# The first four tiles routed by rank alone, and all sixteen low halves of the context subtracted by VectorE

## The chip, the cores and the metric

The kernel runs on one core of one Trainium2 chip. The metric is the time of one execution on the device in microseconds (us), as the median of three runs. The engines are named as the profile names them: PE is TensorE (PEld its weight loads), DVE is VectorE, ACT is ScalarE, POOL is GpSimd, SP is SyncE, whose queue issues most DMAs.

## What is computed

A gated cross-attention block whose attention is a mixture of four experts chosen by token id, followed by a second mixture of experts. `x` is 4 x 512 x 512 in fp32, so there are 2048 tokens; the context `ctx` is one 512 x 512 matrix for each of the four experts and serves as all three of its weights.

```python
def _L0_xattn_ref(hidden_states, token_ids, Wg, Wu, Wd):      # Wg = Wu = Wd = ctx_2048
    tid = jnp.clip(token_ids, 0, VOCAB - 1)
    expert_ids = jnp.minimum(tid // tokens_per_expert, E - 1)
    for e in range(E):
        g = jax.nn.silu(jnp.einsum('bsd,fd->bsf', hidden_states, Wg[e]))
        u = jnp.einsum('bsd,fd->bsf', hidden_states, Wu[e])
        y = jnp.einsum('bsf,df->bsd', g * u, Wd[e])
        out = jnp.where((expert_ids == e)[..., None], y, out)
...
x = x + jnp.tanh(g_xattn[0]) * _L0_xattn_ref(_layernorm(x, axis=-1), itok_BxS_13_99985, ctx_2048, ctx_2048, ctx_2048)
x = x + jnp.tanh(g_ffn[0]) * _L0_ffn_ref(_layernorm(x, axis=-1), L0_ffn_gate_W, L0_ffn_W1, L0_ffn_b1, L0_ffn_W2, L0_ffn_b2)
```

`_L0_ffn_ref` picks two of six small experts for each batch entry and adds their weighted outputs. The change does not touch it.

## The kernel before

**Routing.** The 2048 tokens are sorted by expert into 19 tiles of 128 rows. A chain of small DVE instructions computes for every token its rank within its expert (L498 to L511), from the rank its place in the tile (`pslot`) and its tile (`ptile`, L535 to L551), and two tables of ones and zeros: `slot_hot` (L530 on DVE, L404 on POOL: one compare of 128 columns for each of 16 groups of tokens) and `tile_hot` (L555, L559). PE multiplies the two (`invert`, L917); from the product DVE reads which row of `x` each place of each tile takes (L570 to L573), and a further three instructions (L564 to L567) give `te_i`, the expert of each tile. The semaphore `routed` says that this is done; POOL then gathers the tiles' rows from DRAM with indirect DMAs (L407) into a ring of six buffers, and SP passes on each landing as `x_ready`.

**The context.** Four DMAs of 1 MB bring it. PE transposes it in 16 parts of four transposes each (L988) into four banks in turn. ACT copies each part to the rounded high half `ctx_hi` (L800), and DVE subtracts it from the bank for the low half `ctx_lo` (L622), after which the bank is free for the fourth next part. For parts 0 and 1 PE transposes again and adds the negative of the high half with a matmul by `neg_ident` (L995, L997), and ACT copies the remainder as the low half (L796).

**A tile.** For tile j: `rows_statistics(j)` on DVE (L580 to L582), an inverse root on POOL (L412), `normalise(j)` on DVE, which writes the one buffer `h` (L597), `transpose_h(j)` on PE (L933), high half on ACT (`h_high`, L775), low half on DVE (`h_low`, L602), `first_product(j)` of 12 matmuls (L949), `silu_of(j)` on ACT (L785), `up(j)` on DVE (L614), `transpose_a(j)` (L940), `a_high` (L780) and `a_low` (L608), `second_product(j)` of 12 matmuls (L949), `residual(j)` on DVE (L588 to L592), and a scatter to DRAM by POOL (L418, L419). Each product reads high by high, high by low and low by high halves of the tile and the context.

**Order.** Each engine runs its own list, written out by hand. From tile 2 on PE repeats `tile_step(j)`: `transpose_a(j-1)`, `first_product(j)`, `transpose_h(j+1)`, `second_product(j-1)`; DVE repeats `a_low(j-1)`, `normalise(j+1)`, `residual(j-2)`, `h_low(j+1)`, `up(j)`, `rows_statistics(j+2)`. So `transpose_h(3)` stands in `tile_step(2)` and waits for `normalise(3)`. Ahead of that stands a prologue, with the routing, the context and tiles 0 and 1; it is what the change rewrites. The second mixture of experts follows the 19 tiles.

## Time and profile before

| what | value |
|---|---|
| median of three runs | 296.31 us (296.15 to 296.44) |
| the profiled execution | 296.44 us, of which 294.9 us are its span |
| granted clock of PE, mean | 0.998 |
| PE busy | 279.1 us, 95% of the span |
| DVE busy | 206.6 us, 70% |
| ACT busy | 108.2 us, 37% |
| POOL busy | 65.6 us, 22% |

Times inside the profile count from the start of its span. Busy time overlaps between neighbouring instructions of one engine; where a cost is needed, the distance from one instruction's start to the next one's is the better measure. The time of the execution is 1.5 us more than its span, which lies outside of the profile's instructions.

### The profile page before, as it was taken

How to read it: one execution, taken by the hardware profiler on the slowest of the kernel's cores; microseconds unless marked ns; L12 is line 12 of the kernel's file. 1: busy time of each engine (PE TensorE's matmuls, PEld its weight loads, DVE VectorE, ACT ScalarE, POOL GpSimd, SP SyncE). 2: the span in 40 equal slices, each digit the busy share in tenths (PEclk: the TensorE clock that was granted, in tenths of full speed). 3: DMA queues.
4: the chain of work that ended last, by engine and by line, in shares of the span. 5: the costliest groups of instructions: out<-in, count | busy, mean ns of one | idle time of the engine just before them, and what ended most of it. 6: DMA issues, size and time to landing. Idle time of an engine off the chain costs nothing.

```text
span 294.9 us, 4422 instructions
## 1 busy us (share of the span) xinstructions
PE 279.1 (95%) x1390; PEld 224.6 (76%) x1390; DVE 206.6 (70%) x457; ACT 108.2 (37%) x187; POOL 65.6 (22%) x93
## 2 busy tenths in 40 slices
PE   1977999999999999999999999999999999999995
PEld 0765888888888888877776878877788777878874
DVE  7897687887887899597769555686465854846133
ACT  1682223223223225353254272445442372442010
POOL 3541144545544555333240000000000000000000
PEclk9999999999999999999999999999999999999999
DMA  6941012223245322129515009650486205730003
GB/s 219 369 131 36 0 61 84 74 71 108 76 103 188 104 71 84 61 71 284 191 62 177 4 1 278 234 169 0 122 272 211 75 0 176 218 145 0 1 0 142
DMA packets 21489, 34.44 MB, mean 117 GB/s; under 512 B 1864, under 2 KB 10062, under 8 KB 21468
## 3 DMA queue, kind: packets, MB, share of 16 engines
q1 hardware_dynamic: 18400, 24.16, 25.2%
q0 software_dynamic: 3040, 9.98, 10.4%
q8 instruction: 12, 0.20, 0.3%
q14 instruction: 9, 0.07, 0.1%
q10 hardware_dynamic: 28, 0.02, 0.0%
HBM read 24.97 MB, written 9.19 MB: 116 GB/s over the span
## 4 chain that ended last, share of the span: by engine, by line
PE 84%; DVE 12%; DMA 1%; issue 1%; ACT 1%; POOL 0%; DVEq 0%; ACTq 0%; POOLq 0%; SPq 0%
PE bank L949 33%; PE bank L925 15%; PE bank L926 14%; PE bank L927 14%; PE bank L940 3%; PE bank L933 2%; PE bank L1031 2%; DVE ctx_lo L622 2%; DMA x_ring<-in_x,get_rows 1%; DVE x_odd L706 1%; DVE stats L580 1%; DVE w_lo L686 1%; DVE w_raw L530 1%; DVE a L614 1%; PE bank L1040 1%
## 5 line engine op out<-in xcount | busy, mean ns | idle before, releaser
L925 PE MATMUL bank<-w_lo,ctx_hi 128*128 128x512 f32 (+1 forms) x96 | 38.0, 395 | 0.4 <-DVE ctx_lo L699 0.4
L926 PE MATMUL bank<-w_hi,ctx_hi 128*128 128x512 f32 (+1 forms) x96 | 37.5, 390 | 0.0
L927 PE MATMUL bank<-w_hi,ctx_lo 128*128 128x512 f32 (+1 forms) x96 | 37.4, 390 | 0.0
L686 DVE TENSOR_TENSOR w_lo<-w_raw,w_hi 128x512 fp32r<-128x512 f32 (+2 forms) x24 | 27.7, 1173 | 3.9 <-ACT w_hi L836 3.9
L925 PE MATMUL bank<-ctx_lo,w_hi 128*128 128x512 f32 (+1 forms) x72 | 28.6, 397 | 0.0
L926 PE MATMUL bank<-ctx_hi,w_hi 128*128 128x512 f32 (+1 forms) x72 | 28.2, 392 | 0.0
L927 PE MATMUL bank<-ctx_hi,w_lo 128*128 128x512 f32 (+1 forms) x72 | 28.1, 391 | 0.0
L698 DVE TENSOR_SCALAR ctx_hi<-act,mix 128x512 fp32r<-128x512 f32 x16 | 7.8, 486 | 27.4 <-ACT act L844 27.4
L785 ACT ACTIVATE a<-bank 128x512 f32<-128x512 f32 x19 | 11.4, 598 | 42.6 <-PE bank L949 42.6
L844 ACT ACTIVATE act<-bank,b1T 128x512 f32<-128x512 f32 x16 | 10.9, 688 | 42.3 <-PE bank L927 41.0
L780 ACT ACTIVATE aT_hi<-bank 128x512 fp32r<-128x512 f32 x18 | 10.8, 598 | 41.7 <-PE bank L940 41.6
L836 ACT ACTIVATE w_hi<-w_raw 128x512 fp32r<-128x512 f32 (+2 forms) x24 | 23.6, 1016 | 4.1 <-DMA w_raw<-in_L_ffn_b 3.6
L949 PE MATMUL bank<-ctx_hi,hT_hi 128*128 x80 | 23.5, 416 | 1.4 <-ACT hT_hi L775 1.0
L949 PE MATMUL bank<-ctx_lo,hT_hi 128*128 x80 | 21.7, 392 | 0.3 <-DVE ctx_lo L622 0.3
L925 PEld LDWEIGHTS bank<-w_lo,ctx_hi 128*128 128x128 f32 (+1 forms) x96 | 18.0, 188 | 4.7 <-issue 0.9
L949 PE MATMUL bank<-ctx_hi,hT_lo 128*128 x80 | 21.5, 390 | 0.0
L418 POOL TENSOR_TENSOR x_ring<-x_ring,half 128x1 f32<-128x1 f32 x19 | 10.6, 556 | 48.2 <-DVE x_ring L592 48.2
L949 PE MATMUL bank<-ctx_hi,aT_hi 128*128 x72 | 21.1, 415 | 0.1
L608 DVE TENSOR_TENSOR aT_lo<-bank,aT_hi 128x512 fp32r<-128x512 f32 x18 | 12.3, 685 | 12.5 <-ACT aT_hi L780 12.5
L419 POOL DMA_INDIRECT x_scratch<-x_ring,put_rows x19 | 19.8, 1042 | 5.4 <-POOL x_ring L418 5.4
L927 PEld LDWEIGHTS bank<-w_hi,ctx_lo 128*128 128x128 f32 (+1 forms) x96 | 18.0, 188 | 3.8
L926 PEld LDWEIGHTS bank<-w_hi,ctx_hi 128*128 128x128 f32 (+1 forms) x96 | 18.1, 188 | 3.6
(167 smaller groups left out, 556.8 us busy)
## 6 DMA issues: line engine op xcount, KB each, us to landing
raw_ctx<-in_ctx SPq DMA_DIRECT2D x4, 1024.0 KB, 9.4
w_raw<-in_L_ffn_W SPq DMA_DIRECT2D x8, 512.0 KB
w_raw<-in_L_ffn_W SPq DMA_DIRECT2D x8, 448.0 KB, 4.7
x_even<-x_scratch SPq DMA_DIRECT2D x8, 257.0 KB, 3.5
x_odd<-x_scratch SPq DMA_DIRECT2D x8, 257.0 KB, 3.3
w_raw<-in_L_ffn_W SPq DMA_DIRECT2D x8, 256.0 KB, 3.7
out<-x_even SPq DMA_DIRECT2D x8, 256.0 KB, 2.3
out<-x_odd SPq DMA_DIRECT2D x8, 256.0 KB, 2.1
```

Of the source, the lines that this page charges most:

```text
L418: chain.run(pool.tensor_tensor(deviation, deviation, half[:, 0:1], ALU.pow), apart=True)
L419: pool.indirect_dma_start(x1_rows, bass.IndirectOffsetOnAxis(put_rows[:, j:j + 1], 0), x_ring[:, r * DS:(r + 1) * DS], None).then_inc(scat ...
L608: dve.tensor_tensor(lo[:, :, :].rearrange("p k t -> p (k t)"), bank[:, :], hi[:, :, :].rearrange("p k t -> p (k t)").bitcast(FP32), ALU.su ...
L686: dve.tensor_tensor(part_of(w_lo[s], piece), part_of(w_raw[s], piece), part_of(w_hi[s], piece).bitcast(FP32), ALU.subtract).then_inc(lo_do ...
L780: sc.activation(aT_hi[:, :, :].rearrange("p k t -> p (k t)"), aT_ps[:, :], ACT.Copy).then_inc(aT_hi_done, 1)
L785: sc.activation(a[:, :], z_ps[:, :], ACT.Silu).then_inc(silu_done, 1)
L836: sc.activation(part_of(w_hi[s], piece), part_of(w_raw[s], piece), ACT.Copy).then_inc(hi_done[s], 1)
L844: sc.activation(dst, hid_ps[k % 2][0:rows, :], ACT.Gelu, bias=b1T[0:rows, c, bass.ds(e, 1)]).then_inc(gelu_done, 1)
L925: pe.matmul(dst, s_hi, m_lo, start=first, stop=False)
L926: pe.matmul(dst, s_hi, m_hi, start=False, stop=False)
L927: return pe.matmul(dst, s_lo, m_hi, start=False, stop=last)
L949: return pe.matmul(dst[:, :], src[:, k, :], weights[:, bass.ds(e * (KD * F1) + k * F1, F1)], start=first, stop=last)
```

## The change

The first tile of each expert becomes tile 0 to 3, in the order of the experts, so that tile and expert follow from the rank alone. For it there are tables of their own: `first_slot` (13 compares on DVE, 3 on POOL) and `first_hot` (two DVE instructions), a first `invert`, and the semaphore `first_routed`, after which POOL gathers four tiles. The other 15 tiles are routed later, with `slot_hot` (12 compares on POOL, 4 on DVE), `tile_hot`, `te_i` and a second `invert` spread over the work on tiles 0 to 2. The products of tiles 0 and 1 begin before the context is complete: its transposes 10 to 15 now stand between PE's work on tiles 0 and 1. DVE makes all 16 low halves; the matmuls by `neg_ident` and ACT's two copies are gone. The small tables `gwT` and `b1T` are transposed ahead of the context and copied by ACT, no longer by DVE. Tile 1 gets buffers for its two halves and a bank of its own.

```diff
@@ PE: ahead of the loop
-            for n in range(E * KD):
-                if n == 2:
-                    invert()
-                if n == 8:
-                    turn_small_tables()
...
-            transpose_h(0)
-            pe.wait_ge(routed, 2)
-            e = expert_of(0)
-            pe.wait_ge(ctx_hi_done, E * KD)
...
-            first_product(0, e, low_context)
-            transpose_h(1)
+            spread_gates()
+            turn_small_tables()
+            transpose_ctx(0)
+            transpose_ctx(1)
+            transpose_ctx(2)
+            pe.wait_ge(first_slot_done, IDC)
+            pe.wait_ge(first_hot_done, 2)
+            invert(aT_ps, first_slot, first_hot, E).then_inc(first_rows_done, 1)
+            for n in range(3, 8):
+                transpose_ctx(n)
+            transpose_ctx(8)
+            transpose_ctx(9)
             transpose_h(0)
+            transpose_ctx(10)
+            first_product(0, 0, lambda: transpose_h(1))
+            transpose_ctx(11)
+            transpose_ctx(12)
+            first_product(1, 1)
+            transpose_a(0)
+            transpose_h(2)
+            transpose_ctx(13)
+            transpose_ctx(14)
+            second_product(0, 0)
+            transpose_ctx(15)
+            pe.wait_ge(slot_hot_done, IDC)
+            pe.wait_ge(tile_hot_done, 1)
+            pe.wait_ge(ctx_lo_done, 13)
+            invert(o_ps[0], slot_hot, tile_hot, LATER).then_inc(rows_done, 1)
...
-            tile_step(1)
@@ ACT
-            for n in range(E * KD):
-                sc.wait_ge(ctxT_done, n + 1)
...
-                if 1 <= n <= BY_ACT:
-                    split_low_alone(n - 1)
...
+            for n in range(0, 10):
+                ctx_high(n)
             h_high(0)
+            ctx_high(10)
+            h_high(1)
             silu_of(0)
-            h_high(1)
+            ctx_high(11)
+            ctx_high(12)
             a_high(0)
+            h_high(2)
             silu_of(1)
-            h_high(2)
+            ctx_high(13)
+            ctx_high(14)
+            ctx_high(15)
@@ DVE, after the rank
+            dve.wait_ge(rank_made, 1)
+            for c in range(FIRST_BY_POOL, IDC):
+                dve.tensor_scalar(first_slot[:, c, :], col_h[:, :], rank[:, c:c + 1], None, ALU.is_equal).then_inc(first_slot_done, 1)
...
+            dve.wait_ge(first_rows_done, 1)
+            rows_of(slice(0, E), aT_ps, E, first_routed)
...
+            ctx_low(0)
...
+            ctx_low(4)
...
+            rows_statistics(0)
+            ctx_low(5)
+            normalise(0)
+            rows_statistics(1)
+            ctx_low(6)
             dve.wait_ge(tg_done, 1)
             h_low(0)
             normalise(1)
...
+            h_low(1)
             up(0)
-            h_low(1)
             rows_statistics(2)
...
+            a_low(0)
+            h_low(2)
...
+            up(1)
+            for c in range(LATER_BY_POOL, IDC):
+                dve.tensor_scalar(slot_hot[:, c, :], col_h[:, :], pslot[:, c:c + 1], None, ALU.is_equal).then_inc(slot_hot_done, 1)
...
+            dve.wait_ge(rows_done, 1)
+            rows_of(slice(E, TILES), o_ps[0], LATER, routed)
+            ctx_low(15)
             dve.memset(act_last[:, :], 1.0).then_inc(pads_made, 1)
@@ POOL
+            pool.wait_ge(first_routed, 2)
+            for j in range(E):
+                gather(j, j)
+            inverse_root(0)
+            inverse_root(1)
+            pool.wait_ge(pslot_done, 1)
+            for c in range(LATER_BY_POOL):
+                if c == LATER_BY_POOL // 2:
+                    inverse_root(2)
+                pool.tensor_scalar(slot_hot[:, c, :], col_h[:, :], pslot[:, c:c + 1], None, ALU.is_equal).then_inc(slot_hot_done, 1)
+            inverse_root(E - 1)
             pool.wait_ge(routed, 2)
```

The order of DVE's list where the first tile comes in, before (from the end of the routing on):

```order
L573 CAST put_rows<-rows_f 128x19
L622 TENSOR_TENSOR ctx_lo<-bank,ctx_hi 128x512 [waits ctx_hi_done] x6
L580 BN_STATS stats<-x_ring 128x6 [waits x_ready]
L581 BN_AGGR mv<-stats 128x2 [waits dve_step]
L582 TENSOR_SCALAR ve<-mv 128x1 [waits dve_step]
L622 TENSOR_TENSOR ctx_lo<-bank,ctx_hi 128x512 [waits ctx_hi_done] x2
L597 TENSOR_SCALAR h<-x_ring,mv,rstd 128x512 [waits rstd_ready]
```

Ahead of the first statistics stand six low halves (parts 2 to 7), and eight follow. The same place of DVE's list after the change (`starts` belongs to the routing of the later tiles):

```order
L604 TENSOR_TENSOR ctx_lo<-bank,ctx_hi 128x512 [waits ctx_hi_done] x3
L620 TENSOR_TENSOR starts<-ends,ntile 128x8 [waits dve_step]
L564 BN_STATS stats<-x_ring 128x6 [waits x_ready]
L565 BN_AGGR mv<-stats 128x2 [waits dve_step]
L566 TENSOR_SCALAR ve<-mv 128x1 [waits dve_step]
L604 TENSOR_TENSOR ctx_lo<-bank,ctx_hi 128x512 [waits ctx_hi_done]
L581 TENSOR_SCALAR h<-x_ring,mv,rstd 128x512 [waits rstd_ready]
```

Five low halves (0 to 4) stand ahead of the first statistics now, and eleven follow. DVE's list between `up(1)` and `normalise(3)`, before (L608 is `a_low(1)`, the second L597 row is `normalise(3)`):

```order
L614 TENSOR_TENSOR a<-bank,a 128x512 [waits silu_done]
L580 BN_STATS stats<-x_ring 128x6 [waits x_ready]
L581 BN_AGGR mv<-stats 128x2 [waits dve_step]
L582 TENSOR_SCALAR ve<-mv 128x1 [waits dve_step]
L608 TENSOR_TENSOR aT_lo<-bank,aT_hi 128x512 [waits aT_hi_done]
L597 TENSOR_SCALAR h<-x_ring,mv,rstd 128x512 [waits hT_done,rstd_ready]
```

Twelve rows of the same stretch of DVE's list after the change; ahead of them stand four compares, behind them the rest of L550 to L553, one more low half, a memset, and only then `a_low(1)` and `normalise(3)`:

```order
L658 TENSOR_TENSOR w_raw<-col_h,ptile 128x16x15 [waits dve_step]
L660 TENSOR_TENSOR w_raw<-w_raw,token_h 128x16x15 [waits dve_step]
L604 TENSOR_TENSOR ctx_lo<-bank,ctx_hi 128x512 [waits ctx_hi_done]
L564 BN_STATS stats<-x_ring 128x6 [waits x_ready]
L565 BN_AGGR mv<-stats 128x2 [waits dve_step]
L566 TENSOR_SCALAR ve<-mv 128x1 [waits dve_step]
L664 TENSOR_TENSOR w_raw<-col,ends 128x120
L604 TENSOR_TENSOR ctx_lo<-bank,ctx_hi 128x512 [waits ctx_hi_done]
L668 TENSOR_REDUCE te<-w_raw 128x15 [waits dve_step]
L604 TENSOR_TENSOR ctx_lo<-bank,ctx_hi 128x512 [waits ctx_hi_done]
L671 SCALAR_TENSOR_TENSOR te_i<-w_raw,te 128x15 [waits dve_step]
L550 SCALAR_TENSOR_TENSOR unused<-bank,slot 128x15 [waits rows_done,dve_step]
```

Between `up(1)` and `normalise(3)` there were two steps (statistics and `a_low(1)`); now the whole second half of the routing and the last four low halves lie between them as well. PE's list around the first product, before (L988 are the last two context parts, L933 is `transpose_h(0)`):

```order
L988 MATMUL bank<-ident,raw_ctx 128x128 [waits ctx_lo_done]
L988 MATMUL bank<-ident,raw_ctx 128x128 x3
L933 MATMUL bank<-ident,h 128x128 [waits h_ready]
L933 MATMUL bank<-ident,h 128x128 x3
L944 TENSOR_LOAD te_i [waits routed]
L944 ISA x2
L949 ISA [waits hT_hi_done,ctx_hi_done]
L949 MATMUL bank<-ctx_hi,hT_hi 128x512
```

The same place of PE's list after the change (L1033 is a context part, L972 a `transpose_h`, L990 a product; the first row is context part 9):

```order
L1033 MATMUL bank<-ident,raw_ctx 128x128 [waits ctx_lo_done]
L1033 MATMUL bank<-ident,raw_ctx 128x128 x3
L972 MATMUL bank<-ident,h 128x128 [waits h_ready]
L972 MATMUL bank<-ident,h 128x128 x3
L1033 MATMUL bank<-ident,raw_ctx 128x128 [waits ctx_lo_done]
L1033 MATMUL bank<-ident,raw_ctx 128x128 x3
L990 MATMUL bank<-ctx_hi,hT_hi 128x512 [waits ctx_hi_done,hT_hi_done]
L990 MATMUL bank<-ctx_hi,hT_hi 128x512 x3
L990 MATMUL bank<-ctx_lo,hT_hi 128x512 [waits ctx_lo_done]
L990 MATMUL bank<-ctx_lo,hT_hi 128x512 x3
```

`transpose_h(0)` stands behind ten context parts where it stood behind sixteen, and the first product behind eleven.

## Rows read from the trace of the kernel before

**Rows 1.** Page, part 4: the chain that ended last, shares by engine

```profile
PE 84%; DVE 12%; DMA 1%; issue 1%; ACT 1%; POOL 0%; DVEq 0%; ACTq 0%; POOLq 0%; SPq 0%
```

**Rows 2.** Chain of waits, 11 to 40 us: start us, us, what

```profile
12.12 4.32 DMA x_ring<-in_x,get_rows
...
27.58 0.66 PE bank L940 x4
28.24 2.75 PE bank L949 x12
...
34.62 2.76 PE bank L949 x12
37.38 0.44 PE bank L933 x4
```

**Rows 3.** Busy time of each engine by stretches, us (x instructions), granted clock

```profile
20.90:27.60 6.70, 4.43 (x24) 3.08 (x22) 4.98 (x15) 2.49 (x5) 1.56 (x2) 1.00 0.16 58
...
34.00:40.40 6.40, 6.40 (x33) 5.29 (x32) 5.07 (x12) 1.68 (x3) 2.14 (x3) 1.00 0.00 0
```

**Rows 4.** Timeline of DVE, 12 to 37 us: start us, us, what [idle before]

```profile
13.32 3.08 DVE L622 TENSOR_TENSOR ctx_lo<-bank,ctx_hi 128x512 fp32r<-128x512 f32 x5 [0.47 <-ACT ctx_hi L800]
16.50 0.69 DVE L580 BATCH_NORM_STATS2 stats<-x_ring 128x6 f32<-128x512 f32 x1
...
17.44 0.15 DVE L582 TENSOR_SCALAR ve<-mv 128x1 f32<-128x1 f32 x1
17.51 1.28 DVE L622 TENSOR_TENSOR ctx_lo<-bank,ctx_hi 128x512 fp32r<-128x512 f32 x2
...
29.19 0.48 DVE L635 MEMSET act_last<- 128x512 f32 x1
29.59 0.63 DVE L608 TENSOR_TENSOR aT_lo<-bank,aT_hi 128x512 fp32r<-128x512 f32 x1
...
35.90 0.54 DVE L597 TENSOR_SCALAR h<-x_ring,mv,rstd 128x512 f32<-128x512 f32 x1
...
36.35 0.74 DVE L588 SCALAR_TENSOR_TENSOR x_ring<-bank,tg,x_ring 128x512 f32<-128x512 f32 x1
```

**Rows 5.** Timeline of DVE, 6 to 12 us: the routing

```profile
6.81 0.22 DVE L539 TENSOR_TENSOR w_raw<-w_raw,shift 128x64 f32<-128x64 f32 x1
...
6.94 0.28 DVE L530 TENSOR_SCALAR w_raw<-col_h,pslot 128x128 f16<-128x128 f16 x1
...
9.06 0.47 DVE L559 TENSOR_TENSOR w_raw<-w_raw,token_h 128x304 f16<-128x304 f16 x1
...
9.45 0.89 DVE L530 TENSOR_SCALAR w_raw<-col_h,pslot 128x128 f16<-128x128 f16 x5
10.26 0.30 DVE L564 TENSOR_TENSOR w_raw<-col,ends 128x152 f32<-128x152 f32 x1
...
11.15 0.18 DVE L570 SCALAR_TENSOR_TENSOR unused<-bank,slot 128x19 f32<-128x19 f32 x1
...
11.65 0.17 DVE L573 CAST put_rows<-rows_f 128x19 uint32<-128x19 f32 x1
```

**Rows 6.** Timeline of PE, 6 to 18 us

```profile
6.81 1.97 PE L988 MATMUL bank<-ident,raw_ctx 128*128 128x128 f32 x8 [2.07 <-DMA raw_ctx<-in_ctx]
...
10.40 0.61 PE L917 MATMUL bank<-w_raw 128*128 128x38 f16 x16 [0.24 <-DVE w_raw L530]
...
14.65 0.38 PE L904 MATMUL bank<-gates_in,ones 1*128 1x2 f32 x2
...
15.38 1.97 PE L988 MATMUL bank<-ident,raw_ctx 128*128 128x128 f32 x16
```

**Rows 7.** Timeline of POOL and ACT, 6 to 27 us

```profile
6.74 2.59 POOL L404 TENSOR_SCALAR w_raw<-col_h,pslot 128x128 f16<-128x128 f16 x4 [3.83 <-DVE pslot L526]
...
17.68 0.57 POOL L412 TENSOR_TENSOR rstd<-ve,half 128x1 f32<-128x1 f32 x1 [1.87 <-DVE ve L582]
...
26.21 0.60 ACT L785 ACTIVATE a<-bank 128x512 f32<-128x512 f32 x1 [3.90 <-PE bank L949]
```

More of the change, by code:

```diff
@@ L92, in flamingo_kernel @@
     PREP = TILES - 7
-    BY_ACT = 2
+    LATER = TILES - E
     FC = -(-F2 // P)
@@ L234, in flamingo_kernel @@
         unused = sb("unused", [P, TILES])
-        ended = table(TILES, 2 * E)
-        te = sb("te", [P, TILES])
-        te_i = sb("te_i", [P, TILES], I32)
+        ended = table(LATER, 2 * E)
+        te = sb("te", [P, LATER])
+        te_i = sb("te_i", [P, LATER], I32)
         rows_f = sb("rows_f", [P, TILES])
@@ L532, in _ @@
-            left = list(range(IDC_BY_POOL, IDC))
-            own = own_tile[:, :].unsqueeze(1).to_broadcast([P, E, IDC])
-            chain.wait(ranked)
-            tiled = chain.sign(dve.tensor_tensor(jump[:, :, :], own, by_expert(ntile[:, 0:E]), ALU.is_ge))
-            dve.wait_ge(pslot_done, 1)
-            slot_rows(left.pop())
-            chain.wait(tiled)
-            tiled = chain.sign(dve.tensor_tensor(jump[:, :, :], jump[:, :, :], by_expert(shift[:, :]), ALU.mult))
-            slot_rows(left.pop())
@@ L626, in _ @@
             normalise(1)
-            dve.wait_ge(gwT_done, 1)
-            dve.tensor_copy(gwT[:, :, :], y_ps[:, 0:KD * NE].rearrange("p (k e) -> p k e", e=NE)).then_inc(gwT_copied, 1)
-            for c in range(FC):
-                dve.tensor_copy(b1T[0:FM[c], c, :], y_ps[0:FM[c], (KD + c) * NE:(KD + c + 1) * NE]).then_inc(gwT_copied, 1)
+            ctx_low(7)
+            tiles = chain.sign(dve.tensor_tensor(shift[:, :], starts[:, E:2 * E], ends[:, 0:E], ALU.subtract))
+            ctx_low(8)
@@ L637, in _ @@
-            a_low(0)
-            normalise(2)
-            h_low(2)
-            up(1)
-            rows_statistics(3)
+            chain.wait(tiled)
+            tiled = chain.sign(dve.tensor_tensor(jump[:, :, :], jump[:, :, :], by_expert(starts[:, 0:E]), ALU.add))
+            ctx_low(10)
+            normalise(2)
+            chain.wait(tiled)
+            tiled = chain.sign(dve.tensor_tensor(jump[:, :, :], jump[:, :, :], member[:, :, :], ALU.mult))
+            ctx_low(11)
+            chain.wait(tiled)
```

238 lines of the change are left out of this document (122 added, 116 removed).

## The prediction

> **What bounds the kernel now.** I read the page's chain first, then the chain of waits in order of time, then the timelines of VectorE and TensorE over the first 40 us. The page puts 84% of the chain on TensorE and 12% on VectorE [rows 1]. The chain of waits shows where VectorE's part lies: up to the first transposes of `a` at 27.58 it goes through the gather of tile 0 (12.12, 4.32 long), the statistics, the low halves and the gating, and from there on it is TensorE alone, matmul behind matmul, one tile in 2.76 + 0.44 + 2.76 + 0.44 = 6.4 us [rows 2]. The busy table says the same: between 20.9 and 27.6 TensorE worked 4.43 of 6.7 us, between 34.0 and 40.4 all of 6.4, while VectorE worked 5.07 of these 6.4 [rows 3]. So behind the prologue a shift is carried to the end unchanged, and the change is worth what it moves one milestone. I take `transpose_h(3)`, at 37.38 in the chain [rows 2]: what TensorE has done by then (16 context parts, three first products, one second product) is the same before and after. It needs `normalise(3)`, which ends at 35.90 + 0.54 = 36.44 [rows 4]: 0.94 us of slack, all that VectorE had.
>
> **The start, up to the first statistics.** Ahead of the first gather all sixteen groups of tokens are still compared; what falls away there is the tile arithmetic and the wide table. But TensorE's list now sets the time. The seven small transposes and the gates' matmul take 15.38 - 14.65 = 0.73 us where they stand now; at the start they go ahead of the context. Then come three context parts at the slow pace of the first eight transposes, 1.97 / 8 = 0.25 or, without the last one's tail, 0.21 each, 2.6 us [rows 6]. From 6.81 that gives 10.1. The 16 small matmuls started at 10.40 before [rows 6]. VectorE's compares (13 at 0.16 to 0.20: five starts in 9.45 to 10.26, and 6.94 beside a working POOL [rows 5]) end near 8.1 and are hidden. So the first rows are known about 0.3 to 0.4 us earlier, and the first gather starts at 11.7 to 11.8 in place of 12.12. It took 4.32 us beside the last context DMAs [rows 2], and still would: the first statistics start at 16.2 in place of 16.50 [rows 4]. Bounds: 15.9 (0.3 less contention) and 16.5 (nothing gained). The five low halves ahead of it, from 11.4 on at 0.60, end by 14.8 and are hidden in the same wait.
>
> **VectorE's queue from there to the end of `normalise(3)`.** Starts to starts: a low half costs (3.08 - 0.68) / 4 = 0.60, the statistics 17.51 - 16.50 = 1.01, a normalisation 36.35 - 35.90 = 0.45, the memset 29.59 - 29.19 = 0.40 [rows 4]. `h_low`, `a_low` and `up` have the low half's shape and I take 0.60 for them. Both kernels have four statistics, four normalisations, three `h_low`, two `a_low`, two `up` and the memset: 4.0 + 1.8 + 4.2 + 0.4 = 10.4. Before there were eight low halves (4.8) and four small copies (0.35) besides: 15.6. After there are:
> - eleven low halves (5 to 15), 6.6 (three more than before: two parts that TensorE and ScalarE made, and one that the later rows leave behind the first statistics);
> - seven small steps of the tile arithmetic at about 0.13 (6.81 to 6.94), 0.9;
> - four compares at 0.16, 0.65;
> - the two wide tables at 0.39 (9.06 to 9.45) and a little wait of the first for itself, 0.85;
> - the three steps for `te_i`, 0.89 where they stand in a row (10.26 to 11.15), 0.6 with low halves between;
> - the four steps for the rows, 11.15 to 11.65 and a start, 0.6 [rows 5].
>
> That is 10.4 + 10.2 = 20.6 us, 5.0 more than before. The time before was 36.44 - 16.50 = 19.9, of which 4.3 was waiting. Even with no wait at all VectorE would now end at 16.2 + 20.6 = 36.8, later than 36.44. Where this work was hidden before was the wait for the gather (the routing ended ahead of it); its new cover is the 4.3 us of waits and the 0.94 of slack, and it is as large as both.
>
> **The waits that stay.**
> - `normalise(0)` needs POOL's root: the statistics end 1.1 after their start (17.44 + 0.15), POOL starts 0.09 later and takes 0.57 [rows 4, 7]; one low half covers most, 0.2 is left.
> - `h_low(1)` is the long one. Low half 6 ends near 20.15; then TensorE does context part 10 (0.44), two thirds of the first product (1.85) and `transpose_h(1)` (0.66 to the result, as at 27.58), and ScalarE copies for 0.60 (the length of its `a` at 26.21): 23.8 [rows 2, 7]. VectorE's steps until then end at 23.3. 0.5.
> - `up(0)` behind the rest of the product and the Silu: 0.3.
> - `a_low(0)`: TensorE has two products of 2.76, two context parts and `transpose_a(0)` to do from 20.6 on, which with the copy gives 28.8; VectorE is there at 28.5: 0.3.
> - `normalise(2)` for its root: 0.1.
>
> Sum 1.4. So `normalise(3)` ends at 16.2 + 20.6 + 1.4 + 0.1 (the tail of the last) = 38.3, against 36.44. TensorE would be at `transpose_h(3)` earlier than before: from 20.2 on it has four products of 2.76 and ten groups of transposes of 0.44 (six context parts, four of tiles), the second inversion 0.47, and one wait of 0.6 (the bank of low half 12, which VectorE makes only behind its tables at 33.1). That is 20.2 + 11.1 + 4.4 + 0.5 + 0.6 = 36.8, not 37.38. It waits 1.5 us, restarts with an empty array (0.66 in place of 0.44), and `second_product(1)` then waits some 0.1 to 0.2 more for `residual(0)` to free the bank (0.74 from the end of `normalise(3)` [rows 4]). So the milestone falls 38.3 - 37.38 + 0.2 + 0.2 = **1.3 to 1.5 us late; I take 1.4**. In the next step VectorE has 5.07 of 6.4 us to do, catches up, and no more is lost.
>
> **Edits costed at nothing.** The later gathers: rows for tile 4 are known near 36.4, its gather lands 3.3 to 4.3 later, and its statistics stand at 41.3 in VectorE's list; cover 0.7 at the least. POOL's twelve compares of 0.65 (2.59 / 4 [rows 7]) are done by 31.0, and `tile_hot` by 32.5; cover 1.5. ScalarE's four small copies fit ahead of the first context part, and it is 37% busy. TensorE's matmuls by `neg_ident` stood in waits of the start. Fixed experts for four tiles spare register work, which lay under matmuls.
>
> **Sum.** The profiled execution took 296.44, at the upper end of the three; against it the sum is 297.8, against the median of 296.31 it is **297.7 us**. With the bounds of the landing (-0.3, +0.3) and 0.3 either way for the small steps not seen in this place, the likeliest case's own range is 297.1 to 298.4.
>
> **Two rules weighed.** Compares on POOL and DVE ran side by side: POOL's four took 0.65 each, and a compare that VectorE began amid them at 6.94 took 0.28, one fifth of a microsecond apart from the next [rows 5, 7]. The Trainium skill ("SBUF — State Buffer", Who interferes with whom) says that such an operation of VectorE and one of GpSimd need the same port pair and that the one that comes second is blocked entirely. By the row the twelve compares cost VectorE below 0.1 us; by that rule each two-port operation amid them would wait up to 0.65, some four or five of them, 2 to 3 us more, near 300.
>
> TensorE's gaps are the other place. The rows show two paces of the same transposes: eight in 1.97 us at the start, sixteen in 1.97 later [rows 6], at a granted clock of 1.00 where I looked [rows 3], the upper level of 2.4 GHz. After the change TensorE stands still for 2.6 us ahead of context part 9 (from 15.3 to 17.9) and 1.1 ahead of part 10. If the slow pace returns there, part 10, eight matmuls and `transpose_h(1)` take 2.7 longer on the way to `h_low(1)`, and with 0.2 of a wait swallowed the milestone is 2.5 later: 300.2. The Trainium skill ("TensorE: Matmul & The Clock Gate", What's actually happening) says that an idle array falls back to half its clock; by that rule this can happen here.
>
> **Rivals.**
> - *As costed, VectorE's queue is the bound:* 0.67, 297.7.
> - *Slow pace or port, as above:* 0.11, 299 to 300.2. For it: the gap of 2.6 us is longer than any that the chain shows once TensorE is fast. Against: the sparse stretch from 20.9 to 27.6, with 4.43 of 6.7 us busy [rows 3], left the pace as it was, and the compare at 6.94 was hardly held up.
> - *No change, 296.3:* 0.13. All of VectorE's list hangs on the first statistics, of which some 0.85 of each microsecond reaches `normalise(3)` (the rest goes into waits). 1.4 / 0.85 = 1.6: with the statistics at 14.6 the milestone stands where it was. A landing in 3.5 us and rows known half a microsecond sooner come to 14.9; VectorE's small steps at two thirds of what I take give the rest.
> - *Faster, 295.6:* 0.09. It is an early gather alone. If TensorE takes the first three context parts at the later pace (12 x 0.12 = 1.5 from 7.5 on), inverts at 9.0, the gather starts at 10.7 and lands in 3.0 us beside less of the context, the statistics start at 13.7, 2.5 earlier; 2.5 x 0.85 - 1.4 = 0.7 gained. It begins to pay from 14.6 down. The slow first eight transposes and the 4.32 us of the row speak against it.
>
> The range is 296.5 to 299.4: it leaves out the faster cases, some of no change and most of the slow pace's. What a measurement of this kernel tells from no change is about 0.2%, 0.6 us. Faster by more 0.09, within 0.13, slower 0.78.
>
> **What would show it.** In the changed kernel's profile: the first gather at 11.7 and the first statistics at 16.2; VectorE without gaps above 0.6 us from there to 38; `normalise(3)` ending near 38.3; TensorE idle for some 1.5 us ahead of `transpose_h(3)`, put down to VectorE's `h`; then 6.4 us for a tile. It is wrong if the statistics start before 15, if TensorE doesn't wait at `transpose_h(3)`, or if a product of tile 0 takes twice its 2.76.

## The result, and the profile after

The changed kernel takes **301.19 us** in the median of four executions (298.67, 301.14, 301.24, 301.60) where the kernel before takes 296.25: ratio 1.0139, 95% interval 1.0099 to 1.0179. (A ratio is time over the time of the kernel before; above 1 is slower.) It is slower, as forecast, but 301.2 lies outside the range of 296.5 to 299.4: the loss is 4.9 us where I had 1.4.

The profiled execution took 301.24 us, its span is 299.6 for 294.9, and the page's chain has hardly moved against [rows 1]:

```profile
PE 83%; DVE 9%; DMA 2%; issue 2%; POOL 2%; ACT 1%; ACTq 0%; DVEq 0%
```

It is again the order of time that tells. The chain of waits of the changed kernel, 20 to 46 us, beside [rows 2] (start us, us, what):

```profile
20.26 0.91 PE bank L1033 x4
21.18 3.18 PE bank L990 x8
24.35 0.44 PE bank L972 x4
...
26.60 2.77 PE bank L990 x12
...
39.99 0.66 PE bank L972 x4
...
40.74 4.58 PE bank L990 x12
45.32 0.44 PE bank L981 x4
```

Two lines don't fit the rest. Eight products of tile 0 take 3.18 us, though twelve take 2.77 five microseconds later; and the twelve of `second_product(1)` take 4.58 behind a wait for `h`. `transpose_a(2)`, the group of four behind them, starts at 45.32 where it started at 40.59 (37.38 + 0.44 + 2.77, one tile's pace behind [rows 2]): 4.7 us late, which is the whole difference of the spans.

The busy table of the changed kernel (us of the stretch, then busy us of PE, PEld, DVE, ACT and POOL, then TensorE's granted clock, DMA share, GB/s) answers to [rows 3] and says why:

```profile
18.00:20.90 2.90, 1.94 (x13) 1.48 (x13) 2.77 (x7) 1.19 (x2) 1.23 (x4) 0.94 0.25 81
20.90:22.90 2.00, 2.00 (x7) 1.61 (x6) 2.00 (x6) 0.60 (x1) 2.00 (x4) 0.50 0.00 0
...
24.00:27.60 3.60, 3.60 (x24) 3.06 (x23) 1.90 (x3) 2.17 (x4) 0.00 (x0) 1.00 0.02 5
34.00:40.40 6.40, 4.51 (x39) 3.45 (x37) 6.17 (x18) 1.79 (x3) 1.64 (x2) 1.00 0.08 15
40.40:47.00 6.60, 6.51 (x26) 5.05 (x25) 3.94 (x10) 1.19 (x2) 3.17 (x4) 0.74 0.25 82
```

The granted clock is 0.50 between 20.9 and 22.9, the lower of TensorE's two levels (1.2 GHz), and again for part of the last row. In the kernel before it was 1.00 from 20.9 to 27.6 and from 34.0 to 40.4 [rows 3], and it is 1.00 from 40.4 to 47.0 as well. The falls come while TensorE is at work, but behind stretches in which it did little: 1.94 of 2.9 us busy ahead of the first, 4.51 of 6.4 ahead of the second.

TensorE's own timeline shows the gaps and the longer durations (in brackets the idle time before, and what ended it):

```profile
12.37 4.50 PE L1033 MATMUL bank<-ident,raw_ctx 128*128 128x128 f32 x20 [0.46 <-DVE ctx_lo L604]
...
18.02 0.66 PE L1033 MATMUL bank<-ident,raw_ctx 128*128 128x128 f32 x4 [1.15 <-DVE ctx_lo L604]
...
20.26 0.91 PE L1033 MATMUL bank<-ident,raw_ctx 128*128 128x128 f32 x4 [0.95 <-DVE ctx_lo L604]
20.83 2.06 PE L990 MATMUL bank<-ctx_hi,hT_hi 128*128 128x512 f32 x4
...
39.99 0.66 PE L972 MATMUL bank<-ident,h 128*128 128x128 f32 x4 [1.59 <-DVE h L581]
40.74 1.81 PE L990 MATMUL bank<-ctx_hi,aT_hi 128*128 128x512 f32 x4
```

Four products take 2.06 and 1.81 us here, where the same lines take 1.17 at the upper clock. The twenty context transposes from 12.37 on still run at the slow pace of the first eight in [rows 6], and end 1.5 us later than I had them. And VectorE, beside [rows 4]:

```profile
16.26 0.69 DVE L564 BATCH_NORM_STATS2 stats<-x_ring 128x6 f32<-128x512 f32 x1 [1.19 <-SPq L349]
...
25.46 0.69 DVE L587 TENSOR_TENSOR hT_lo<-bank,hT_hi 128x512 fp32r<-128x512 f32 x1 [1.96 <-ACT hT_hi L809]
...
39.40 0.54 DVE L581 TENSOR_SCALAR h<-x_ring,mv,rstd 128x512 f32<-128x512 f32 x1
```

The first statistics start at 16.26 (forecast 16.2), `normalise(3)` ends at 39.94 (38.3), and the wait ahead of `h_low(1)` is 1.96 (0.5): the first fall sits in that wait.

### The profile page after: what moved, and what is told of

Read it like the earlier page. It is cut to its first block, busy times and chain, and to the rows that moved or that the text cites. A ratio compares the mean times of both kernels' runs of the same rounds, so it can differ in the third digit from the quotient of the medians.

```text
span 299.6 us, 4366 instructions
## 1 busy us (share of the span) xinstructions
PE 283.7 (95%) x1396; PEld 229.0 (76%) x1396; DVE 208.1 (69%) x465; ACT 108.3 (36%) x189; POOL 72.6 (24%) x104
## 4 chain that ended last, share of the span: by engine, by line
PE 83%; DVE 9%; DMA 2%; issue 2%; POOL 2%; ACT 1%; ACTq 0%; DVEq 0%
PE bank L990 32%; PE bank L964 14%; PE bank L965 14%; PE bank L966 14%; PE bank L981 3%; PE bank L972 2%; PE bank L1085 2%; DMA b_rows<-in_L_ffn_b 2%; PE bank L1033 2%; POOL x_ring L426 1%; DVE x_odd L740 1%; DVE ctx_lo L604 1%; DVE stats L564 1%; DVE w_lo L720 1%; DVE aT_lo L593 1%
## 5 line engine op out<-in xcount | busy, mean ns | idle before, releaser
L990 PE MATMUL bank<-ctx_hi,hT_hi 128*128 (+1 forms) x80 | 24.4, 428 | 0.5 <-ACT hT_hi L900 0.5
L990 PE MATMUL bank<-ctx_lo,hT_hi 128*128 (+1 forms) x80 | 22.2, 400 | 0.0
L990 PE MATMUL bank<-ctx_hi,aT_hi 128*128 (+1 forms) x72 | 21.7, 425 | 0.2
L990 PE MATMUL bank<-ctx_hi,hT_lo 128*128 (+1 forms) x80 | 21.6, 392 | 0.0
L426 POOL DMA_INDIRECT x_ring<-in_x,get_rows x19 | 19.2, 1011 | 9.6 <-DVE put_rows L553 6.1
```

The costliest lines, as they stand in the source:

```text
L426: pool.indirect_dma_start(x_ring[:, r * DS:r * DS + D], None, x_rows, bass.IndirectOffsetOnAxis(get_rows[:, j:j + 1], 0)).then_inc(gathere ...
L990: return pe.matmul(dst[:, :], src[:, k, :], weights[:, bass.ds(e * (KD * F1) + k * F1, F1)], start=first, stop=last)
```

## The experiments

Theory A: the loss is VectorE's queue as forecast, about 1.4 us, and two falls of TensorE's clock with a price of 1.5 to 1.8 each. Rival B: the queue alone, longer than I had counted. Rival C: the two extra low halves, or the way the routing is split, cost something of their own. Each kernel was timed against the kernel before on the same chip; ratios are to that. The kernel before had medians from 296.39 to 297.06 there.

**1. Filling the gaps.** `keep_busy` issues identity transposes whose result nobody reads, in places where TensorE waits anyway.

```diff
+            def keep_busy(bank, count):
+                for _ in range(count):
+                    pe.transpose(bank[:, 0:P], ident[:, :], ident[:, :])
...
             spread_gates()
+            keep_busy(o_ps[3], 9)
             turn_small_tables()
...
+            pe.wait_ge(tg_done, 1)
+            keep_busy(z_ps, 12)
             transpose_ctx(9)
             transpose_h(0)
+            keep_busy(z_ps, 8)
             transpose_ctx(10)
...
                 first_product(j, e)
+                if j == 2:
+                    pe.wait_ge(hT_lo_done, 3)
+                    keep_busy(hT_ps, 12)
                 transpose_h(j + 1)
```

`fill_all` has all four, `fill_last` the last alone, `fill_early` the first three.

> The changed kernel with TensorE kept at work in all its gaps: 9 transposes of the identity behind the gates' matmul, 12 ahead of context part 9, 8 ahead of part 10 and 12 ahead of transpose_h(3). Theory A (two falls of the clock cost 1.7 and 1.8 us on top of VectorE's queue): both are gone, the granted clock is 1.00 from some 11 us on, and the time is what the queue alone costs, 297.7 to 298.2 us, with a scatter between runs of some tenths of a microsecond in place of 3. Theory B: 301 us and as scattered as before.

> The changed kernel with twelve more transposes of the identity on TensorE (into a bank that is then overwritten) ahead of the wait for normalise(3) in tile_step(2). Nothing of the result depends on them. Theory A (the wait of 1.59 us there lets TensorE's clock fall, and second_product(1) takes 4.58 us in place of 2.76): the clock stays at its upper level behind the wait, second_product(1) takes 2.8 us, and the time falls by 1.8 to about 299.4 us. Theory B (the wait alone costs, the slow product has another reason, such as the gathers and scatters beside it): no change, 301.2 us, and the product still takes 4.6.

> The changed kernel with the identity transposes in TensorE's three early gaps alone (9, 12 and 8), none ahead of transpose_h(3). Two clock falls with a price each: the first is gone (1.6 us), the second behind the gap at transpose_h(3) stays with 1.8 us: 299.6 to 300.2 us where fill_all is 298.16, ratio 1.009 to 1.011, and the profile shows second_product(1) at 4.6 us in the chain. If the second fall comes only after a first one (or after a thin start), the clock holds and the time is that of fill_all, 1.004.

`fill_all`: **298.16 us** (six executions, 298.14 to 298.45), ratio 1.0041 (1.0025 to 1.0056). The granted clock is 1.00 in every stretch of the busy table above, and the scatter is gone. Its chain of waits, with the same work at the same places:

```profile
20.99 1.85 PE bank L990 x8
...
38.50 0.66 PE bank L972 x4
39.25 2.98 PE bank L990 x12
42.22 0.44 PE bank L981 x4
```

Eight products take 1.85 for 3.18, twelve 2.98 for 4.58. In `fill_all` `normalise(3)` ends at 38.44, and `transpose_a(2)` starts at 42.22: 1.63 later than in the kernel before. That is the queue alone. The changed kernel is 1.49 later still at `transpose_h(3)` (39.99 for 38.50) and 1.60 longer in the twelve products (4.58 for 2.98). 1.63 + 1.49 + 1.60 = 4.7, the whole difference of the spans. By rival B the fillers would have changed nothing.

`fill_last`: 299.31, six executions at 297.96, 298.12, 299.24, 299.38, 300.41 and 300.46, ratio 1.0083 (1.0056 to 1.0110). That the median is the 299.4 I expected is luck: it lies in the middle one of three pairs, with mean granted clocks of 0.999 and 1.000, 0.992, and 0.987 to 0.988. Only the fastest was profiled. It has no fall, though its early gaps (1.39 and 0.95 us idle) are as empty as in the changed kernel; what the two slowest had, with the last gap filled, isn't seen.

`fill_early`: 298.73, at 297.93, 297.97, 298.01, 299.44, 299.61 and 299.87, ratio 1.0070 (1.0044 to 1.0095): groups 1.6 us apart, so one fall comes or doesn't. Its profiled execution had the one behind `transpose_h(3)`: the clock in the busy table is 1.00 up to 37.00, and then

```profile
37.00:40.40 3.40, 1.95 (x9) 1.51 (x10) 3.30 (x8) 1.00 (x2) 0.73 (x2) 0.94 0.28 77
40.40:44.00 3.60, 3.60 (x13) 2.81 (x13) 1.84 (x5) 0.00 (x0) 2.82 (x4) 0.58 0.19 73
```

The twelve products take 4.57 in its chain.

So the second fall can come alone, and I was wrong to expect it every time. The first comes without the second in the profiles of `late_lows` and `moved_no_fill` below.

**2. The changed kernel again**, for more executions.

> The changed kernel as it is, more executions of it. Theory of the two clock falls with a price each: executions stand in groups at 298.0 to 298.7 (no fall), 299.2 to 300 (one) and 300.9 to 301.6 (two), with spans some 1.5 us apart and a mean granted clock near 0.998, 0.993 and 0.988. Rival (the 301.2 is a fixed cost and 298.67 a stray): all within 0.3% of 301.2.

298.07, and five from 301.13 to 301.65, ratio 1.0138 (1.0098 to 1.0178). The one at 298.07 has a span of 296.5 at a granted clock of 1.000, that of `fill_all`; the others have 299.5 to 300.0 at 0.983 to 0.989. The 298.67 of the first four had 297.0 at 0.994. By their times eight of ten executions have both falls, and without them the changed kernel would take what I forecast, plus 0.4. The group with one fall that I had expected at 299.2 to 300 has no execution in it.

**3. VectorE's queue.** `late_lows` moves the last two low halves and the memset behind the work of tiles 2 and 3; `late_lows_fill` adds the three early fillers.

```diff
-            ctx_low(14)
...
-            ctx_low(15)
-            dve.memset(act_last[:, :], 1.0).then_inc(pads_made, 1)
             for j in range(2, PREP):
...
                 up(j)
+                if j == 2:
+                    ctx_low(14)
+                    ctx_low(15)
+                if j == 3:
+                    dve.memset(act_last[:, :], 1.0).then_inc(pads_made, 1)
```

> The changed kernel with VectorE's low halves 14 and 15 moved behind up(2) and its memset behind up(3), so that 1.6 us of work leave the queue ahead of normalise(3). Theory A (VectorE's queue is what TensorE waits for at transpose_h(3)): the wait of 1.6 us there all but vanishes, and with it the second fall of the clock; the milestone is 1.6 + 0.2 + 1.8 earlier and the time 297.5 to 298 us, with the first fall left in it. Theory C (the later routing of tiles 4 to 18 holds TensorE: its bank, te_i or the late gather of tile 4): the wait moves to the first product of tile 3 or 4 or to the statistics of tile 4, and the time stays at 300 us or more.

> late_lows and the transposes of the identity in the three gaps of the prologue (9, 12 and 8). If the queue and the two falls of the clock are all that made the changed kernel slow, nothing of its loss is left, and TensorE's shorter list ahead of transpose_h(3) shows: transpose_h(3) at about 36.8 in place of 37.38, time 295.6 to 296.2 us. If the prologue has a loss of its own (context parts between the products, the late gather), it stays at 297 us or above.

`late_lows`: 299.26 (297.38 to 299.67), 1.0072 (1.0053 to 1.0092), 1.3 us more than the 298 that I had written down at the most. The profiled execution is the fastest of the six. In it the wait at `transpose_h(3)` is gone and the early fall is not: the granted clock is 0.51 from 18.0 to 21.5, behind 2.04 us of idling, and `transpose_a(2)` comes 0.8 later than in `late_lows_fill` (41.18 for 40.42). Four executions took 299.2 to 299.7 at 0.986 to 0.989; what they had more isn't seen.

`late_lows_fill`: 296.63 (296.46 to 296.99), 0.9990 (0.9978 to 1.0001). With 1.6 us taken out of the queue `transpose_h(3)` starts 1.84 us earlier than in `fill_all` (36.66 for 38.50), and with no fall the loss is gone. It doesn't become a gain, as the chain shows:

```profile
36.66 0.66 PE bank L974 x4
...
37.41 3.01 PE bank L992 x12
40.42 0.44 PE bank L983 x4
```

`transpose_h(3)` comes 0.7 earlier than in [rows 2], but it takes 0.66 for 0.44, the products behind it start another 0.09 later and take 3.01 for 2.77, and `transpose_a(2)` is 0.2 earlier only.

**4. One part of the change alone:** the low halves, in the kernel before.

```diff
-    BY_ACT = 2
+    BY_ACT = 0
-            dve.tensor_scalar(neg_ident[:, :], col[:, :], part[:, 0:1], -1.0, ALU.is_equal, ALU.mult).then_inc(consts_made, 1)
-                pe.wait_ge(ctx_lo_by_act, BY_ACT)
```

> The kernel before with one part of the change alone: VectorE subtracts all sixteen low halves of the context, TensorE and ScalarE make none; the routing stays whole. My step (VectorE's queue, low halves hidden by the gather): the two more subtractions lie in the wait for the first gather, of which all but some 0.2 us is covered; 0 to +0.4 us against the kernel before, ratio 1.000 to 1.0015, with the first statistics at 16.5 to 16.8 us. Rival (the low halves themselves are what the change costs): +1.2 us (two subtractions of 0.60) or more, ratio 1.004 or more.

297.37 (296.71 to 297.83), ratio 1.0020 (1.0008 to 1.0032). More than I had said. VectorE's timeline:

```profile
12.07 3.28 DVE L621 TENSOR_TENSOR ctx_lo<-bank,ctx_hi 128x512 fp32r<-128x512 f32 x5
...
16.36 1.29 DVE L621 TENSOR_TENSOR ctx_lo<-bank,ctx_hi 128x512 fp32r<-128x512 f32 x2 [0.16 <-ACT ctx_hi L799]
17.56 0.69 DVE L579 BATCH_NORM_STATS2 stats<-x_ring 128x6 f32<-128x512 f32 x1
```

Eight low halves stand ahead of the first statistics here. With 0.7 us of waits among them they fill more than the wait for the gather: the statistics start 1.06 later than in [rows 4] and `transpose_h(3)` 0.97 later (38.35), and the medians lie 0.9 apart (297.37 for 296.43). In that place the two low halves aren't hidden. In the changed kernel five stand ahead of the statistics and 1.19 us of waiting is left, so there they don't cost by this way, but as three of the eleven in the queue behind, two of which `late_lows_fill` took out with the memset. Rival C has no cost left to explain: in `fill_all` VectorE's list up to `normalise(3)` takes what its pieces add up to within half a microsecond, and `late_lows_fill`, with the split routing, no fall and a shorter queue, has the time of the kernel before.

**5. A wait of the same length in the kernel before.** Idle statistics of 128x512 ahead of `normalise(3)`, into a buffer of their own (`before_delay`) or into the one that is there (`before_delay_b`); `before_shift` has the new buffer alone, with nothing that uses it.

```diff
+        spare = sb("spare", [P, 6])
...
                 a_low(j - 1)
+                if j == 2:
+                    for _ in range(3):
+                        run(dve.bn_stats(spare[:, :], ring_row(2, 0, D)))
                 normalise(j + 1)
```

> The kernel before with work of no use on VectorE: three more statistics of 128x512 (0.7 us each, each waits for its own end), 2.2 us, ahead of normalise(3), as much as makes VectorE 1.3 us late for transpose_h(3), where the changed kernel is 1.6 late. The wait alone: h is there at 38.65 for 36.44, TensorE is ready at 37.38, so 1.3 and a restart of 0.3: +1.5 to +1.6 us, ratio 1.0052. If TensorE's clock falls behind such a gap, as in the profile of the changed kernel, the 12 products after it show 4.6 us for 2.76 in the chain and the time is +3.3 to +3.5 us, ratio 1.0115, and runs lie scattered between the two. If it is the sparse start of the changed kernel that makes the clock fall behind the gap, this one shows no fall: 1.0052 without scatter.

> before_delay again, without its confound: the three idle statistics write into the tile that is there already, so that no buffer moves in SBUF (with the 24 bytes of the first version every group of 12 products took 2.79 to 2.81 us for 2.76 to 2.77, over the whole span). Queue theory: transpose_h(3) at 39.07 for 37.38, the chain's transpose_a(2) at 43.0 for 40.59, so +1.9 to +2.4 us by the trace of the first version, products back at 2.76: ratio 1.006 to 1.008. Rival (what made before_delay 5.2 us slower is the wait itself, given on to later stages): ratio 1.017 again.

> The kernel before with a buffer of 128x6 f32 that nothing uses, put behind act_last, so that every later buffer stands 24 bytes (or the next multiple of 32) higher: no instruction is added. If the place alone makes products slower, each group of 12 takes 2.79 to 2.81 us and the time is +2.5 to +3 us, ratio 1.009 to 1.010. If it was something else in before_delay (the writes of its idle statistics), no change: 1.000.

`before_delay` took 301.62 (301.31 to 302.08), 1.0172 (1.0155 to 1.0188), with no fall of the clock in the profile: outside all that I had written down. The chain of waits gave the reason away, first its own and then that of `before_shift`:

```profile
43.43 2.79 PE bank L953 x12
...
46.66 2.80 PE bank L953 x12
```

```profile
41.22 2.79 PE bank L950 x12
...
44.45 2.81 PE bank L950 x12
```

Every group of products takes 2.79 to 2.81 us in place of 2.76 to 2.77, to the end. `before_shift`: 299.40 (299.28 to 299.70), 1.0095 (1.0071 to 1.0120), 3 us for a buffer that nothing touches: where the later buffers start is what counts. `before_delay_b`, without it: **298.41** (298.13 to 298.96), 1.0063 (1.0047 to 1.0080), products back at 2.76, and

```profile
39.08 0.66 PE bank L936 x4
...
39.93 3.00 PE bank L952 x12
42.93 0.44 PE bank L943 x4
```

1.7 late at `transpose_h(3)`, 2.3 at `transpose_a(2)`, 2.0 in the time. A late `h` costs the kernel before the same as the changed one: its lateness, and 0.6 for the restart (in `fill_all` 0.5, in the prediction 0.4). But no execution of the two, five and six, has a mean granted clock under 0.997 (one with a fall in `fill_early` has 0.991 to 0.994), though TensorE waited 1.28 us there. A wait of that length alone didn't bring the fall. It isn't quite the changed kernel's: that one is 1.59 long, and TensorE was 4.51 of the 6.4 us up to its end busy, here 5.12. Which of the two makes the difference wasn't tried.

**6. When the first gather lands.** `fill_tables` is `fill_all` with the small tables behind the first inversion; `ctx_last` moreover holds the last context load back.

```diff
-            turn_small_tables()
             transpose_ctx(0)
...
+            turn_small_tables()
             for n in range(3, 8):
```

```diff
                 for r in range(RING):
                     announce(k, r)
+                    if k == 0 and r == 0:
+                        load_context(E - 1)
```

> fill_all with the seven small transposes (gate weights and first biases) behind the first inversion, not ahead of the context, and ScalarE's copies of them behind high half 2. The first three context parts, the first inversion and the first gather come some 1.1 us earlier (first statistics at 15.2 to 15.6 for 16.33). Queue theory: all that VectorE does up to normalise(3) moves by that, 0.7 to 1.1 us earlier, and the time by as much: 297.1 to 297.5 us where fill_all is 298.16, ratio to the kernel before 1.0005 to 1.002. Rival (the wait at transpose_h(3) hangs on what VectorE waits for later, not on the gather): no change against fill_all, 1.004.

> fill_tables with the load of the last expert's context held back until the first gather has landed. In fill_tables the gather went out at 10.62 and landed at 16.27 (5.65 us), in the changed kernel at 11.93 and 16.2 (4.3), before at 12.12 and 16.44: theory, all land when the 4 MB of context are through, whose 16 DMA engines are full until then. Then here the first gather takes 2.5 to 3.5 us and lands at 13.2 to 14.2, the first statistics start by 14.5, normalise(3) and the end come 1.5 to 2.5 us earlier than in the runs of fill_tables without a clock fall (298.1): 295.8 to 296.6 us, ratio 0.996 to 1.000. Rival (the gather's time is its own, with the descriptors on GpSimd): landing 16.2 as before, 298 us, ratio 1.004 or more; or the held load is then late for context part 12 and TensorE waits there.

`fill_tables`: 299.35, at 297.97, 298.17, 299.18, 299.51, 299.66 and 300.19, ratio 1.0082 (1.0057 to 1.0106). The gather goes out 1.3 us earlier than in the changed kernel, and nothing comes of it (ScalarE's copies of the small tables move too, behind high half 2). The chain of waits:

```profile
10.62 5.65 DMA x_ring<-in_x,get_rows
...
16.33 0.71 DVE stats L564
```

The busy table of `fill_tables` over the gather's time, and then that of `ctx_last`:

```profile
10.60:14.20 3.60, 3.05 (x22) 2.07 (x21) 3.17 (x11) 2.75 (x5) 2.97 (x3) 1.00 1.05 390
```

```profile
10.60:14.20 3.60, 3.06 (x21) 2.04 (x20) 3.19 (x11) 2.73 (x6) 2.94 (x3) 1.00 0.60 166
```

With all of the context under way the DMA engines are full (share 1.05, 390 GB/s) and the rows land at 16.27, whether their gather went out at 10.62 as here or at 12.53 as in `fill_all`; those of the kernel before, out at 12.12, land at 16.44 [rows 2]. With a quarter of it held back the share is 0.60, and the first statistics start at 14.35, by VectorE's timeline:

```profile
14.35 0.69 DVE L568 BATCH_NORM_STATS2 stats<-x_ring 128x6 f32<-128x512 f32 x1 [0.56 <-SPq L351]
```

`transpose_h(3)` comes at 36.60 for 38.50. So the theory of the landing holds. Of the time less arrived than I had written down: 297.44 in twelve executions (296.13 to 298.29), 1.0028 (1.0014 to 1.0042), though the profiled span of 294.6 is 1.8 under that of `fill_all`. Spans vary from 294.5 to 295.9, without a low clock, and in seven of the twelve the time is 2.2 to 2.6 us more than the span. `fill_tables` and `routing_early`, with all four fillers as well, have up to 2.7 and `fill_all` 1.7 to 1.9; every other kernel has 1.5 to 1.8. So part of what is missing lies outside the span. Why is open.

`fill_tables` shows one thing more: its profiled execution has the early fall, in spite of the fillers. TensorE's timeline:

```profile
14.30 1.47 PE L1038 MATMUL bank<-ident 128*128 128x128 f32 x12
18.09 0.65 PE L1033 MATMUL bank<-ident,raw_ctx 128*128 128x128 f32 x4 [2.31 <-DVE ctx_lo L604]
```

The twelve identity transposes are over at 15.77, and the gap, 2.31 us, comes behind them. The granted clock is 0.53 from 18.7 to 22.3, and `transpose_h(3)` starts at 39.81, 1.3 later than in `fill_all`. Four of its six executions have a mean of 0.994 and take 299.18 or more.

**7. Moving the rest of the routing.** `routing_early`: `fill_all`, with the tile arithmetic and VectorE's four later compares between the first compares and the first rows, and three of GpSimd's compares ahead of the gathers (two in the kernels after it). There VectorE's timeline of the changed kernel has

```profile
11.00 0.16 DVE L550 SCALAR_TENSOR_TENSOR unused<-bank,slot 128x4 f32<-128x4 f32 x1 [2.72 <-PE bank L956]
```

`all_moved`: this, the edits of `fill_tables`, `ctx_last` and `late_lows`, and the three early fillers; `moved_no_fill`: `all_moved` without any filler.

```diff
+            chain.wait(slots)
+            owned = chain.sign(dve.tensor_single_scalar(ptile_i[:, :], rank_i[:, :], SHIFT, ALU.logical_shift_right))
...
+            later_row(12)
...
+            tiled = chain.sign(dve.tensor_tensor(ptile[:, :], own_tile[:, :], ahead[:, :], ALU.add))
             dve.wait_ge(first_rows_done, 1)
             rows_of(slice(0, E), aT_ps, E, first_routed)
```

> fill_all with the rest of the routing (tile tables, the four later compares of VectorE) moved into VectorE's wait for the first inversion, 8.1 to 11.6, and three of GpSimd's compares ahead of the gathers. Queue theory: of the work between the first statistics and normalise(3) some 1.3 us (eight small operations of 0.08 to 0.2 and 0.65 of compares) is gone, normalise(3) at 36.6 for 37.91, transpose_h(3) 1.1 to 1.3 us earlier, nothing else changed: 296.9 to 297.1 us where fill_all is 298.16, ratio 1.0000 to 1.0008. Rival (VectorE waits for ScalarE or TensorE instead): under 0.4 us of it arrive, ratio 1.003 or more.

> All that helped together: identity transposes in the three early gaps, small tables behind the first inversion, last context load behind the first gather, the rest of the routing in VectorE's early wait, low halves 14 and 15 and the memset behind up(2) and up(3). By the queue theory TensorE becomes the bound from the first product on and transpose_h(3) comes by 35.2 to 36 for 37.38 in the kernel before: 294.8 to 296 us, ratio 0.993 to 0.998, faster than both kernels. Rival (TensorE's restarts and waits for residual(0) give it back, as in late_lows_fill): 296.3 to 296.7.

> all_moved without any identity transpose that is there only to keep TensorE busy: small tables behind the first inversion, last context load behind the first gather, rest of the routing in VectorE's early wait, low halves 14 and 15 and the memset later. If the falls come from the thin stretch between parts 9 and 10 whatever the rest, they stay: 295 plus 1.4 in most executions, 296.2 to 296.8, scattered. If less waiting is enough, 294.8 to 295.5 as all_moved.

`routing_early`: 297.51 (297.19 to 298.33), 1.0041 (1.0027 to 1.0054). `transpose_h(3)` starts at 37.54 for 38.50: 0.96 of the 1.3 removed, by the profile; the span is 0.9 shorter and the median 0.65, on another chip. By its ratio it is no better than `fill_all`, which is what I had written down for the rival: the kernel before had a median of 297.06 beside `fill_all` and 296.41 here. So the profile shows the gain, and the times don't. `all_moved`: **294.98** (294.76 to 295.54), 0.9952 (0.9936 to 0.9968), faster than both kernels. `moved_no_fill`: 296.38 (294.88 to 296.86), 0.9974 (0.9953 to 0.9995), five executions at 294.9 to 295.4 and seven at 296.4 to 296.9; the profiled one had the early fall, its eight products at 3.31 in the chain. `all_moved` reads

```profile
20.01 1.84 PE bank L1007 x8
...
35.41 0.44 PE bank L989 x4
...
35.92 3.00 PE bank L1007 x12
38.92 0.44 PE bank L998 x4
```

No wait is left at `transpose_h(3)`, and `transpose_a(2)` comes 1.7 earlier than in the kernel before. The clock does fall in this execution, the fastest of its kernel, and earlier than in any above:

```profile
12.00:15.50 3.50, 3.50 (x18) 3.46 (x19) 2.54 (x5) 1.84 (x4) 2.64 (x3) 0.53 0.46 126
```

Here it costs nothing that shows: the chain runs through the gathers and the first root meanwhile (11.55 to 17.12), and the three executions with a mean clock of 0.991 or 0.992 took 294.76 to 294.89, the other three 295.07 to 295.54. So a kernel with the change in it can be faster than the one before. How much of that is owed to the change and how much to the later context load, which the kernel before could have as well, these runs don't tell apart.

## Why the prediction was right and wrong

- *First gather at 11.7 to 11.8, first statistics at 16.2.* Near in number (11.93 and 16.26), by luck in part. I took the 4.32 us "beside the last context DMAs" for the gather's duration, and it is what was left until the context had landed: 5.65, 3.74 and 4.32 us all end at 16.3 to 16.4. My rival "faster" rested on a gather at 10.7 that lands in 3.0 us; `fill_tables` made exactly that gather, and it took 5.65.
- *VectorE's queue, 20.6 us of work and 1.4 of waits.* Right to half a microsecond each. `fill_all` shows 38.44 - 16.33 = 22.1 with about 1.0 of waits, so 21.1 of work; `normalise(3)` at 38.44 against 38.3 forecast.
- *The wait of 1.5 at `transpose_h(3)`, the milestone 1.4 late.* Right: 1.59 idle, and without the falls `transpose_a(2)` is 1.63 late, the span 1.5 longer, and the time 1.1 to 1.2 by the median and the ratio of `fill_all`, beside which the kernel before scattered from 296.17 to 297.78.
- *The step that failed* is what the sum took for TensorE's clock: nothing. It has every product at 2.76 and the restart behind the wait at 0.2, that is, the upper level throughout. In the runs two falls to the lower level add 1.49 and 1.60 us to the queue's 1.63. The first I had seen as the rival "slow pace", in its place (the gap ahead of part 9, then part 10, the first product and `h_low(1)`), but with only a share of a chance of 0.11, because the stretch from 20.9 to 27.6, with 4.43 of 6.7 us busy [rows 3], had left the pace alone. It came in eight of ten executions by their times, behind idle pieces of 1.15 and 0.95 us where I had 2.6 and 1.1. Its price I had at 2.5 on top of the queue, and it was 1.49. The second fall is nowhere in the prediction: I had written a wait of 1.5 us ahead of `transpose_h(3)` and an empty array behind it, and did not ask about the clock in this gap as I had in the other. That this rival's 300.2 is only 1.0 short of the measured time is luck: one fall with too high a price stands there for two.
- *The rule of the Trainium skill* ("TensorE: Matmul & The Clock Gate", What's actually happening), that an idle array falls back to half its clock, pointed the right way: granted 0.50 in the rows of the changed kernel. But from 7 us on the array was never idle for longer than 1.6 us at a stretch there, and in `before_delay_b` it was idle for 1.28 without a fall, so being idle is not the whole of it.
- *The port.* The Trainium skill ("SBUF — State Buffer", Who interferes with whom) says that the second of two operations that need the shared port pair is blocked entirely. It cost nothing that shows. POOL's compares ran from 20.2 to 24.0, and VectorE beside them kept its pace: `normalise(1)` and the low half behind it start 0.49 apart (0.45 in the sum), a low half and a small step take 0.74 (21.21 to 21.95; 0.73 in the sum):

```profile
20.72 0.57 DVE L581 TENSOR_SCALAR h<-x_ring,mv,rstd 128x512 f32<-128x512 f32 x1
21.21 0.68 DVE L604 TENSOR_TENSOR ctx_lo<-bank,ctx_hi 128x512 fp32r<-128x512 f32 x1
21.81 0.22 DVE L630 TENSOR_TENSOR shift<-starts,ends 128x4 f32<-128x4 f32 x1
21.95 0.68 DVE L604 TENSOR_TENSOR ctx_lo<-bank,ctx_hi 128x512 fp32r<-128x512 f32 x1
```

What stays open is what decides a fall. With the same instructions eight executions of the changed kernel have the times of two falls, one has none (298.07), and 298.67 at a mean clock of 0.994 lies between. A wait of 1.28 in the kernel before had no fall behind it in eleven executions, one of 1.59 in `fill_early` had one in three of six, by their times. That identity transposes in the gaps prevent the falls is shown where they stand at the end of the gap: in the 37 executions of `fill_all`, `late_lows_fill`, `routing_early` and `ctx_last` no mean clock is under 0.997. In `fill_tables`, where 2.31 us of a gap lie behind them, they didn't. A threshold is not shown.

## What to carry to other kernels

A wait that a change puts in front of TensorE costs its own length and perhaps a stretch at half clock behind it: price both at each such wait, and look whether executions lie in groups. The price depends on what TensorE does in that stretch: 1.3 to 1.6 us here where it ran products for most of it, 0.8 in `late_lows`, nothing that shows in `all_moved`, where the end waited for something else. Before moving work to start a transfer earlier, read the DMA share at that time: while it was near 1 here, the gather ended with the context's loads, whenever it had started. When a shared list gets longer, look for an idle stretch ahead of it that its pieces could fill; 2.7 us of one were there.

## What was not expected of the hardware

A buffer of 24 bytes per partition that nothing uses, put ahead of others, made each group of twelve matmuls take 2.79 to 2.81 us in place of 2.76 to 2.77 and the kernel 1.0095 times as long (1.0071 to 1.0120). Which operand's place does it wasn't tried. And executions of one kernel can fall into groups, with the granted clock as the only difference that the records show: 298.07 and 301.13 to 301.65 for the changed kernel. There is also a scatter without any low clock: beside `fill_all` the spans of the kernel before lie between 294.6 and 296.2.
